# Experts of a routed feed-forward layer: channels as 128 and 64, tokens in twelves of 120, narrowing and transposes between widening matmuls

## The reference

```python
capacity = int(CAPACITY_FACTOR * N / E)      # int(1.25 * 9216 / 8) = 1440
...
h = jax.nn.gelu(jnp.einsum('ecd,edf->ecf', buf[:E], w1) + b1[:, None, :], approximate=False)
o = jnp.einsum('ecf,efd->ecd', h, w2) + b2[:, None, :]
```

## Time and profile before

| | us |
|---|---|
| median of 3 runs (lowest, highest) | 7712.14 (7709.46, 7726.1) |
| the profiled execution, its own time | 7705.95 |
| its span, first to last instruction | 7704.4 |
| TensorE busy in the span | 6614.5 |
| mean granted TensorE clock | 0.907 |

### The profile page before, as it was taken

The page is one execution under the profiler, slowest core; times in us unless marked ns, Lnnn a source line. Parts: engine busy times, 40 slices in busy tenths (PEclk is TensorE's granted clock), DMA queues, the critical chain, the costliest instruction groups (busy, mean ns, idle before and its releaser), DMA issues. The chain is left out here.

```text
span 7704.4 us, 233323 instructions
## 1 busy us (share of the span) xinstructions
PE 6614.5 (86%) x87595; PEld 4183.7 (54%) x87595; DVE 4720.3 (61%) x7714; ACT 3174.2 (41%) x5336; POOL 2305.7 (30%) x2558
## 2 busy tenths in 40 slices
PE   6698999999997677599999982499779999999977
PEld 4254555555554554276767672377445555555546
DVE  6688888888883400132323236011579999999976
ACT  2066666767674133122222220122344444444432
POOL 0011111111111000000000000300339999999961
PEclk8699999999998788699999985799889999999986
DMA  3211111111113423301010012211651111111123
GB/s 116 76 38 38 35 38 36 38 37 38 37 33 79 121 59 92 97 1 28 1 28 19 1 53 83 74 54 42 190 176 37 38 36 37 37 37 38 36 64 105
DMA packets 415540, 428.73 MB, mean 56 GB/s; under 512 B 76977, under 2 KB 387801, under 8 KB 409659
## 3 DMA queue, kind: packets, MB, share of 16 engines
q1 hardware_dynamic: 332859, 339.62, 15.4%
q0 software_dynamic: 62400, 59.16, 3.1%
q10 hardware_dynamic: 19712, 21.53, 0.9%
HBM read 253.47 MB, written 166.55 MB: 55 GB/s over the span
## 5 line engine op out<-in xcount | busy, mean ns | idle before, releaser
L628 DVE TENSOR_REDUCE softmax_part_max<-softmax_ring 128x1 f32<-128x512 f32 (+1 forms) x2880 | 1679.3, 632 | 333.9 <-PE softmax_ring L536 276.2
L2456 POOL TENSOR_TENSOR retention_decayed<-retention_third,retention_decay_table 128x384 f32<-128x384 f32 x1728 | 1690.5, 1005 | 106.1 <-ACT retention_third L2478 101.6
L2437 DVE TENSOR_TENSOR retention_decayed<-retention_scores,retention_decay_table 128x768 f32<-128x768 f32 x1728 | 1654.1, 957 | 89.9 <-PE retention_scores L2398 57.5
L668 ACT ACTIVATE softmax_probs<-softmax_scores 128x768 f32<-128x768 f32 x1728 | 1392.4, 810 | 676.4 <-PE softmax_scores L558 604.1
L536 PE MATMUL softmax_ring<-softmax_k_next,softmax_q_next 96*32 96x512 bf16 (+1 forms) x11520 | 1117.6, 377 | 185.0 <-issue 81.8
L2398 PE MATMUL retention_scores<-retention_q_half,retention_k_piece 96*32 96x384 bf16 x20736 | 1184.8, 325 | 36.6 <-DMA retention_v_piece<-ret_v 29.6
L2478 ACT COPY retention_third<-retention_scores 128x384 f32<-128x384 f32 x1728 | 826.6, 478 | 891.3 <-PE retention_scores L2398 891.3
L2410 PE MATMUL retention_sums<-retention_decayed,retention_v_piece 128*32 128x288 f32 x13824 | 1182.7, 406 | 3.3 <-POOL retention_decayed L2456 0.6
L2398 PEld LDWEIGHTS retention_scores<-retention_q_half,retention_k_piece 96*32 96x32 bf16 x20736 | 628.5, 95 | 516.8 <-DVE retention_decayed L2437 42.4
L569 PE MATMUL softmax_sums<-softmax_probs,softmax_v_piece 128*32 128x192 f32 x13824 | 884.5, 330 | 11.3 <-issue 10.6
L558 PE MATMUL softmax_scores<-softmax_q_third,softmax_k_piece 99*32 99x384 bf16 x13824 | 887.9, 332 | 2.9 <-DMA softmax_v_piece<-rope_v 1.8
(11 more groups left out here) (301 smaller groups left out, 6831.2 us busy)
## 6 DMA issues: line engine op xcount, KB each, us to landing
ret_v<-ret_proj_values SPq DMA_DIRECT2D x8, 1728.0 KB, 8.8
retention_v_piece<-ret_v SPq DMA_DIRECT2D x144, 96.0 KB
softmax_q_third<-rope_q SPq DMA_DIRECT2D x192, 54.0 KB
softmax_q_next<-rope_q POOLq DMA_DIRECT2D x64, 162.0 KB, 3.9
softmax_k_piece<-rope_k SPq DMA_DIRECT2D x192, 54.0 KB
softmax_k_next<-rope_k POOLq DMA_DIRECT2D x64, 162.0 KB, 5.8
ret_q<-ret_proj_parts SPq DMA_DIRECT2D x48, 216.0 KB, 2.8
ret_k<-ret_proj_parts SPq DMA_DIRECT2D x48, 216.0 KB, 3.0
```

Source lines behind the costliest of these rows:

```text
L628: nc.vector.reduce_max(part_max[:, j, c:c + 1], ring[m % 2][:, 0:CHUNKS[c][1]], axis=X)\
L668: nc.scalar.activation(probs[n % 4][:, :].rearrange("p (c q) -> p c q", c=2), scores[n % 2][:, :, 0:QC], ACT.Exp, scale=scale).then_inc(ex ...
L2437: nc.vector.tensor_tensor(weights[n % 4][:, 0:2 * QC].rearrange("p (c q) -> p c q", c=2), scores[n % 2][:, 0:2, 0:QC], table[:, table_at(n ...
L2456: nc.gpsimd.tensor_tensor(weights[n % 4][:, 2 * QC:HALF], third[n % 3][:, :], table[:, at:at + QC], ALU.mult)\
```

## The change

Contraction of the widening: in place of channels 0 to 95 and 96 to 191, `turned` now holds channels 0 to 127 in part 0 and channels 64 to 191 in part 1, so channels 64 to 127 are there twice. A block f of hidden channels takes a matmul of 128 rows from part f % 2 and one of 64 rows from the other part: for an even f the channels 128 to 191, on partitions 64 to 127 of part 1; for an odd f the channels 0 to 63, on partitions 0 to 63 of part 0. The matching rows of w1 are loaded as `w1` and `w1_over` by six transfers from the same array, in runs of 512 bytes. Within a group of blocks all 128-row matmuls come first and then the 64-row ones, each of which increments `hid_full`.

Tokens: 12 tiles of 120, three chunks of four tiles, W still 480. Narrowing has 12 x 6 matmuls an expert with 120 stationary columns.

Order on TensorE: a chunk's step is widening of four blocks of the next chunk, narrowing of two tiles, one burst of four transposes of the next expert, widening of the other two blocks, narrowing of two tiles, one burst of transposes. The next chunk of the last one is the first of the next expert, so there are two `turned`. The tokens have a semaphore and a load of their own, issued when the last transposes of an expert are done; the nine weight transfers are issued when its results are taken. The loops run three pairs of experts with a hint on the back edge, and the last pair is written out.

```diff
@@ -24,6 +24,11 @@
+
+def hinted(nc, eng, start, end):
+
+    return nc.Fori(start, end, engines=bass.OrderedEngineSet([eng.engine]), hint_back_edge=True)
...
@@ -2145,59 +2150,85 @@
+    OVER = C - P
-    TP = 96
+    TP = 120
...
-    PAIRS = [(t, min(2, TPC - t)) for t in range(0, TPC, 2)]
-    NP = len(PAIRS)
...
-        w1 = [sb(f"w1_{i}", [HC, 2, F], F32) for i in range(2)]
+        w1 = [sb(f"w1_{i}", [P, FT // 2, 2, P], F32) for i in range(2)]
+        w1_over = [sb(f"w1_over{i}", [P, FT // 2, P], F32) for i in range(2)]
...
-        turned = sb("turned", [HC, 2, capacity], F32)
+        turned = [sb(f"turned{i}", [P, 2, capacity], F32) for i in range(2)]
...
-        loaded = [sem(f"loaded{i}") for i in range(2)]
-        stored = [sem(f"stored{i}") for i in range(2)]
+        tokens_in, weights_in, stored = ([sem(f"{n}{i}") for i in range(2)] for n in ("tokens_in", "weights_in", "stored"))
...
-        LOADS = 5
-        NT, NH, NO = 2 * CHUNKS, FT * CHUNKS, NP * CHUNKS
+        NT, NH, NO = 2 * CHUNKS, FT * CHUNKS, 2 * CHUNKS
+        WEIGHT_DMAS = 9
...
+        def each_expert(eng, body):
+
+            with hinted(nc, eng, 0, E // 2 - 1) as pair:
+                for i in range(2):
+                    body(pair * 2 + i, i, True)
+            for i in range(2):
+                body(E - 2 + i, i, i == 0)
+
+        def chunk_after(e, i, c):
+
+            return (e, i, c + 1) if c + 1 < CHUNKS else (e + 1, 1 - i, 0)
+
+        def bank_of(i, c, f):
+            return hid_bank[((i * CHUNKS + c) * FT + f) % 4]
+
...
+            def load_tokens(e, i):
+                sp.dma_start(tokens[i][:, :, :], expert_rows(e)).then_inc(tokens_in[i], 16)
+
+            def load_weights(e, i):
+                low, high = (w_in[e, :, half, :].rearrange("c (n r f) -> c n r f", r=2, f=P) for half in range(2))
+                for to, of in [(w1[i][0:HC, :, 0, :], low[:, :, 0, :]), (w1[i][HC:P, :, 0, :], high[0:P - HC, :, 0, :]),
+                               (w1[i][0:P - HC, :, 1, :], low[OVER:HC, :, 1, :]), (w1[i][P - HC:P, :, 1, :], high[:, :, 1, :]),
+                               (w1_over[i][OVER:P, :, :], high[HC - OVER:HC, :, 0, :]), (w1_over[i][0:OVER, :, :], low[0:OVER, :, 1, :]),
+                               (b1[i][:, :], b_in[e, :, :]), (w2[i][:, :, :], w_out[e, :, :, :]),
+                               (b2[i][:, :], b_out[e, :].partition_broadcast(TP))]:
+                    sp.dma_start(to, of).then_inc(weights_in[i], 16)
...
-            load(0, 0)
-            load(1, 1)
-            with sp.Fori(0, E // 2 - 1) as pair:
+            for i in range(2):
+                load_tokens(i, i)
+                load_weights(i, i)
+            with hinted(nc, sp, 0, E // 2 - 1) as pair:
                 for i in range(2):
-
-                    sp.wait_ge(out_done, (pair * 2 + i + 1) * NO)
-                    load(pair * 2 + 2 + i, i)
+                    e = pair * 2 + i
+
+                    sp.wait_ge(tr_full, (e + 1) * NT)
+                    load_tokens(e + 2, i)
+
+                    sp.wait_ge(out_done, (e + 1) * NO)
+                    load_weights(e + 2, i)
...
-            with pool.Fori(0, E // 2) as pair:
+            with hinted(nc, pool, 0, E // 2) as pair:
...
@@ -2207,88 +2238,118 @@
+            def turn(e, i, g, first=False):
+                c, part = divmod(g, 2)
+                if g == 0:
+                    pe.wait_ge(tokens_in[i], (e - i + 2) * 8)
+                if not first or g >= 2:
+
+                    pe.wait_ge(tr_copied, e * NT + g - 1)
+                for t in range(TPC):
+                    last = nc.tensor.transpose(tr_bank[part][:, t * TP:(t + 1) * TP],
+                                               tokens[i][:, c * TPC + t, part * OVER:part * OVER + P], identity[0:TP, 0:TP])
+                last.then_inc(tr_full, 1)
+
+            def widen(e, i, c, fs, first=False):
+                if fs[0] == 0:
+                    if c == 0:
+                        pe.wait_ge(weights_in[i], (e - i + 2) * (WEIGHT_DMAS * 8))
+                    pe.wait_ge(tr_copied, e * NT + 2 * c + 2)
+                chunk = slice(c * W, (c + 1) * W)
+                for f in fs:
+                    if not first or f >= 4:
+
+                        pe.wait_ge(hid_done, e * NH + c * FT + f - 3)
+                    nc.tensor.matmul(bank_of(i, c, f)[:, 0:W], w1[i][:, f // 2, f % 2, :], turned[i][:, f % 2, chunk],
+                                     start=True, stop=False)
+                for f in fs:
+                    part = slice(0, OVER) if f % 2 else slice(OVER, P)
+                    nc.tensor.matmul(bank_of(i, c, f)[:, 0:W], w1_over[i][part, f // 2, :], turned[i][part, 1 - f % 2, chunk],
+                                     start=False, stop=True).then_inc(hid_full, 1)
+
+            def narrow(e, i, c, half):
+                if half == 0:
+                    pe.wait_ge(hid_done, e * NH + (c + 1) * FT)
+
+                pe.wait_ge(out_done, e * NO + c * 2 + half - 1 if c or half else e * NO)
+                for k in range(2):
+                    t = 2 * half + k
+                    for f in range(FT):
+                        last = nc.tensor.matmul(out_bank[half][0:TP, k * C:(k + 1) * C],
+                                                hidden[(i + c) % 2][:, f, t * TP:(t + 1) * TP], w2[i][:, f, :],
+                                                start=(f == 0), stop=(f == FT - 1))
+                last.then_inc(out_full, 1)
+
+            def body(e, i, following):
+                for c in range(CHUNKS):
+                    ahead = following or c + 1 < CHUNKS
+                    if ahead:
+                        widen(*chunk_after(e, i, c), range(0, 4))
+                    narrow(e, i, c, 0)
+                    if following:
+                        turn(e + 1, 1 - i, 2 * c)
+                    if ahead:
+                        widen(*chunk_after(e, i, c), range(4, FT))
+                    narrow(e, i, c, 1)
+                    if following:
+                        turn(e + 1, 1 - i, 2 * c + 1)
 
...
-                    narrow(e, i, CHUNKS - 1)
+            for g in range(NT):
+                turn(0, 0, g, first=True)
+            widen(0, 0, 0, range(0, 4), first=True)
+            widen(0, 0, 0, range(4, FT), first=True)
+            each_expert(pe, body)
...
+            def activate(e, i, c, first=False):
+                if c == 0:
+                    act.wait_ge(weights_in[i], (e - i + 2) * (WEIGHT_DMAS * 8))
+                if not first:
+
+                    act.wait_ge(out_full, e * NO + c * 2 - 2)
+                for f in range(FT):
+                    act.wait_ge(hid_full, e * NH + c * FT + f + 1)
+                    nc.scalar.activation(hidden[(i + c) % 2][:, f, :], bank_of(i, c, f)[:, 0:W], ACT.Gelu, bias=b1[i][:, f:f + 1])\
+                      .then_inc(hid_done, 1)
+
+            def body(e, i, following):
+                for c in range(CHUNKS):
+                    if following or c + 1 < CHUNKS:
+                        activate(*chunk_after(e, i, c))
+
+            activate(0, 0, 0, first=True)
+            each_expert(act, body)
...
+            def copy_turned(e, i, g):
+                c, part = divmod(g, 2)
+                dve.wait_ge(tr_full, e * NT + g + 1)
+                nc.vector.tensor_copy(turned[i][:, part, c * W:(c + 1) * W], tr_bank[part][:, 0:W]).then_inc(tr_copied, 1)
+
+            def take_results(e, i, c, half):
+                if c == 0 and half == 0:
+                    dve.wait_ge(weights_in[i], (e - i + 2) * (WEIGHT_DMAS * 8))
+
+                    dve.wait_ge(stored[i], (e - i) * 8)
+                dve.wait_ge(out_full, e * NO + c * 2 + half + 1)
+                t = c * TPC + 2 * half
+                nc.vector.tensor_tensor(results[i][:, t:t + 2, :],
+                                        out_bank[half][0:TP, 0:2 * C].rearrange("p (t c) -> p t c", c=C),
+                                        b2[i][:, :].unsqueeze(1).to_broadcast([TP, 2, C]), ALU.add).then_inc(out_done, 1)
+
+            def body(e, i, following):
+                for c in range(CHUNKS):
+                    for half in range(2):
+                        take_results(e, i, c, half)
+                        if following:
+                            copy_turned(e + 1, 1 - i, 2 * c + half)
+
+            for g in range(NT):
+                copy_turned(0, 0, g)
+            each_expert(dve, body)
```

More of the change, by code:

```diff
@@ L2209, in _ @@
         def _(pe):
-            def transposes(e, i):
-                for g in range(NT):
-                    c, half = divmod(g, 2)
-                    pe.wait_ge(tr_copied, e * NT + max(g - 1, 0))
-                    for t in range(TPC):
-                        last = nc.tensor.transpose(tr_bank[g % 2][0:HC, t * TP:(t + 1) * TP],
-                                                   tokens[i][:, c * TPC + t, half * HC:(half + 1) * HC], identity[0:TP, 0:TP])
-                    last.then_inc(tr_full, 1)
```

(20 more changed lines are left out.)

42 lines of the change are left out of this document (removed).

## The result

| | before | after |
|---|---|---|
| median, us (lowest to highest, 4 runs each) | 7713.21 (7709.46 to 7726.1) | 7615.09 (7607.52 to 7621.83) |
| ratio of the medians, 95% interval | | 0.987 (0.9856 to 0.9884) |
| span of the profiled execution, us | 7704.4 | 7620.3 |

A forecast was written before the change was run, and what follows sets the result against it. The experts' stage was taken as a chain of TensorE matmuls, passes times distance between starts. 46.8 + 58.0 - 19.2 + 9.0 + 4.6 - 0.7 = 98.5 us off 7712.1 gave 7613.6 us, range 7600 to 7650.

The forecast's parts named there:

- narrowing: Experts' narrowing matmuls: 36 passes fewer an expert at 0.1625 us each, 46.8 us less.
- pairs: Widening's 64-row matmuls run side by side on two row halves, 72 slots become 54 an expert: 58.0 us less.
- entering and leaving: Switching into and out of the short matmuls on TensorE: 0.40 us a group, 48 groups, 19.2 us more.
- transposes: TensorE's token transposes, 24 in bursts of four for 30 held up by VectorE's copies: 9.0 us less.
- earlier start: First expert: TensorE waits for tokens alone and transposes while weights come; widening 4.6 us earlier, ends 2.5 and 6.
- clock at the start: First expert's first 48 widening passes: 2.67 us lost to a clock of 0.50, left as it is, ends 1 and 4.
- first chunk's stall: First chunk has nothing to put between its activations of 0.66 us: 0.5 us more.
- What hides the rest: TensorE's wait for ScalarE to empty banks 0 and 1: covered by half a narrowing (3.9 us) and four transposes.
- no pairing: Rival: short widening matmuls stand one behind the other, 58.0 us more, 7671.6 us; chance 0.07.
- The weight load: Rival: the load of 24 more columns sets the narrowing, 20 ns a pass, 23 us more, 7637 us; chance 0.03.
- The stall behind ScalarE: Rival: ScalarE gets banks late, TensorE waits 1 to 1.5 us a chunk, 7638 to 7650 us; chance 0.06.
- The granted clock: Rival: half-filled passes and gaps take TensorE's clock to 0.50; all passes so, about 8010 us; slower has chance 0.02.

The follow-up runs named there:

- one row half: Changed kernel with every 64-row matmul on partitions 64 to 127, so no two stand on different halves: stage 470.86 us, median 7676.07 us, ratio to before 0.9948.
- transposes in one row: Changed kernel with all 24 transposes of the next expert, and VectorE's copies, in one row behind the second chunk: stage 422.56 us, median 7618.31 us.

## Why the prediction held, point by point

| term | forecast | measured | by |
|---|---|---|---|
| narrowing | -46.8 | -46.8 | main part of the kernel before, tiles of 120 alone |
| pairs | -58.0 | -57.8 | rows of both groups, one row half |
| entering and leaving | +19.2 | +19.2 | 0.40 in the rows and by the main part, 48 times |
| transposes | -9.0 | -9.7 | 42 bursts of 0.412 = 17.3, from 27.0 |
| earlier start | -4.6 | -3.3 | widening 14.81 us after the first issue, 18.07 before |
| clock at the start | 0 | -2.7 | first eight passes 3.33 us, as later ones; 2.67 over before |
| first chunk's stall | +0.5 | +1.3 | the table load |
| last add | +0.2 | +0.2 | 558 ns for 354 |

The measured column adds up to -99.6; the stage, with the last add's end, fell by 99.8. From that end to the next stage's first issue it is 9.65 us before and 10.55 after, 0.9 more, which the forecast had at nothing. With tiles of 120 alone it is 11.1, so neither the new order of the work nor the pairs are needed for it; why the last store takes longer wasn't tried. In the transposes, 0.9 of the 9.7 us are the longer waits where the loop goes back; they are gone with transposes in one row too (the longest wait for VectorE is 0.4 us there), and no run tells whether by the loop's hint or by something else.

*Right, and for the reasons given:* the stage was a chain of passes without gaps, so each term could be a count times a distance, and the distances came from rows of the same form elsewhere in the kernel. The rows of L1382 and its neighbours had shown pairing and its price; 1.81 and 1.01 us for the two groups, forecast as 1.8 and 1.0, are the result. An expert's three steps were forecast at 50.0 and take 50.0.

*Mis-sized:* the earlier start, and the clock at the start. The tokens were expected after half of the loading time; all their rows bind the transposes, and these began 9.56 us after the first issue, not near 8. The clock's cost at the start was carried over as it was. In the profile before, the clock stood at 0.50 up to 4923, 10 us behind the first transpose; after, it was full by the first widening, 5 us behind it. In the kernel before with tiles of 120, where the code gives no reason for it, it came sooner too, and the two profiles of the changed kernel differ in it as well (24 transposes and their waits 5.25 and 4.69 us). So no run ties this term to the change, and the profile that the forecast was read from may simply have had the late case. What sets the moment stays open. These errors, with those of the stall, the transposes and the tail, nearly cancel, and that is luck.

*Wrong in the reason:* "What hides the rest" named half a narrowing as the cover of the wait for banks 0 and 1. Taken away, nothing happens; ScalarE starts inside the group, and is in time by 0.05 us. The half narrowing covers a wait only where ScalarE has to wait for the whole group. And the 0.5 us of the first chunk was put on activations without cover, where a table load of 1.28 us stood: the list of groups before has four of them, but there they ran beside transposes. The Trainium skill ("ScalarE: Activation LUTs", "What ACT_TABLE_LOAD costs") gives 1283 ns for the load itself, and the trace agrees with 1.28 us; of the 1380 ns of drain that it adds for a switch nothing shows here, where ScalarE had stood idle for 237 us ahead of the load and its first activation follows 0.01 us behind.

*Rivals:* no pairing would have been 470.9 us of stage, and it is what the kernel with one row half gives. The weight load doesn't set the narrowing. The stall behind ScalarE doesn't appear even uncovered, though only by 0.05 us. The granted clock stayed at 1.00 from 4926 to 5320 us, with half of the widening matmuls on half of the rows.

## What to carry to other kernels

Where one engine runs without gaps, look for the same form of instruction elsewhere in the trace, take the distance between starts, and price the edges of a group too: here 0.40 us a group, 48 times, which took 19 of the 58 us that pairing brought. Before naming a cover, compare when the other engine can begin, not how long it takes in all. At the start of a stage, work that comes earlier but leaves a pause behind it can lose in clock what it won in time, as it did in one profile here. To tell kernels apart by less than the whole execution varies, find a stretch of the trace that repeats in profiles of the same code: the main part here repeats to 0.01 us, the stage to 0.7, the execution to some 10.

## What the runs showed of the hardware

- 64-row float32 matmuls on the two row halves ran side by side in both orders that were tried: 1.81 us for four with halves alternating, 1.82 us with two and two, 3.42 us on one half.
- A weight load of 0.183 us for 120 columns lay beside matmuls of the same rows that started every 0.1626 us, the same distance as with the 0.163 us load of 96 columns.
- Going from 128-row to 64-row matmuls and back cost 0.40 us in all, also next to other long passes: 8.78 us for 22 groups more, 4.8 for 12 fewer.
- The granted clock fell during a pause of 3.35 us that followed some 5 us of transposes, and the next eight passes took 6.00 us for 3.33. Behind a pause of 2.17 us it fell in one profile (four passes 3.49 us for 1.81); behind one of 2.10 in another it did not.
- The load of ScalarE's table, 1.28 us, stood in front of the first activation and held TensorE 1.28 us; with a one-column Gelu ahead of it the idle time was gone.
